# A three-layer GCN with attention behind it: the neighbour sums go in sets of 16 steps, without row copies

## The reference

```python
def _conv(x, row, col, edge_type, edge_weight, W, b):
    deg = segment_sum(ones, col); deg_inv_sqrt = where(deg > 0, deg ** -0.5, 0)
    norm = deg_inv_sqrt[row] * deg_inv_sqrt[col] * edge_weight
    xw = einsum('ni,tio->tno', x, W)                 # 4 tables of N x 128
    x_j = xw[edge_type, col] * norm[:, None]
    return leaky_relu(segment_sum(x_j, row, num_segments=N) + b, 0.01)
z1 = _conv(x, ...W1); z2 = _conv(z1, ...W2); z3 = _conv(z2, ...W3)
x = _layernorm(x + (x + z1 + z2 + z3) / 4)
# attention: alpha = leaky_relu(a_src[src] + a_dst[dst], 0.2), softmax over the edges of a dst,
# out = segment_sum(alpha * xp[src]) + bias
x = _layernorm(x + attention(x))
```

## Time and profile before

| | |
|---|---|
| median of the runs | 8943.34 us |
| span of the profiled execution | 11925.3 us |
| POOL busy | 6395.8 us (54%) |
| PE busy / PEld busy | 5307.0 (45%) / 4105.0 us (34%) |
| DVE busy | 4574.2 us (38%) |
| ACT busy | 3992.0 us (33%) |
| gathers of the layers (L737) | 4743 x 946 ns |
| copies g_step (L912) | 5580 x 390 ns |

### The profile page before, as it was taken

One profiled execution on the slowest core, in us unless ns is written; L12 is line 12 of the kernel. 1 busy time (PEld: TensorE's weight loads), 2 busy tenths in 40 slices (PEclk: granted clock), 3 DMA queues, 4 the chain that ended last, 5 costly groups with the idle time before them and its releaser, 6 DMA issues.

```text
span 11925.3 us, 149378 instructions
## 1 busy us (share of the span) xinstructions
PE 5307.0 (45%) x32765; PEld 4105.0 (34%) x32766; DVE 4574.2 (38%) x12940; ACT 3992.0 (33%) x12236; POOL 6395.8 (54%) x6521
## 2 busy tenths in 40 slices
PE   5843434434533434343433434343444444444444
PEld 4632322223322323232322323232344444444444
DVE  9952222222322212222322222222555555555556
ACT  6522222222322222222322222222455454445455
POOL 1656566565456565656466565656344444444443
PEclk9975655656655655565655556555566666666666
DMA  1011111111221111111211111111122222222222
GB/s 47 35 42 43 41 44 43 41 44 41 65 55 44 40 44 40 44 40 44 76 42 44 40 44 40 44 40 44 49 69 70 68 71 69 69 68 69 70 69 65
DMA packets 432687, 612.42 MB, mean 51 GB/s; under 512 B 232038, under 2 KB 249491, under 8 KB 432539
## 3 DMA queue, kind: packets, MB, share of 16 engines
q0 software_dynamic: 208832, 428.96, 13.7%
q1 hardware_dynamic: 223707, 182.02, 4.6%
HBM read 437.29 MB, written 51.28 MB: 41 GB/s over the span
## 4 chain that ended last, share of the span: by engine, by line
another core or an unknown queue 48%; DVE 16%; issue 15%; PE 8%; ACTq 5%; DVEq 4%; ACT 3%; POOL 0%; DMA 0%; POOLq 0%; SPq 0%
DVEq L1604 3%; PE bank L1196 3%; ACT g_step L912 3%; ACTq L896 2%; DVE a_miss L1717 2%; PE wide L1196 2%; DVE g_hot L1620 2%; ACTq L912 1%; DVE acc L1634 1%; DVE a_max L1722 1%; DVE lo_hot L1262 1%; DVE acc L1788 1%; PE bank L1191 1%; DVE v_hot L1387 1%
## 5 line engine op out<-in xcount | busy, mean ns | idle before, releaser
L737 POOL DMA_INDIRECT g_rows<-gcn_table,rec_idx x4743 | 4487.1, 946 | 2894.2 <-ACT g_step L912 1484.6
L912 ACT ACTIVATE g_step<-g_rows,rec_w 128x128 f32 x5580 | 1791.5, 390 | 5679.7 <-remote 4618.4
L762 POOL DMA_INDIRECT a_roll<-gat_table,src_plane x1612 | 1524.6, 946 | 1801.0 <-ACT a_cand L937 1375.4
L1634 DVE TENSOR_TENSOR acc<-acc,bank 128x512 f32 x930 | 637.9, 686 | 3828.8 <-remote 3238.9
L1191 PE MATMUL bank<-zeros 1*128 1x512 bf16 x930 | 490.9, 528 | 2909.9 <-DVE acc L1634 2104.6
L1196 PE MATMUL bank<-g_step,g_hot 128*128 128x128 f32 x7440 | 1621.7, 386 | 128.4 <-issue 50.6
L1196 PEld LDWEIGHTS bank<-g_step,g_hot 128*128 128x128 f32 x7440 | 1391.8, 280 | 487.9 <-issue 487.9
L1222 PE MATMUL bank<-a_msg,a_hot 128*128 128x130 f32 x3608 | 798.9, 389 | 1648.7 <-DVE a_msg L1768 1635.0
L1222 PEld LDWEIGHTS bank<-a_msg,a_hot 128*128 128x128 f32 x3608 | 685.6, 283 | 1786.3 <-DVE a_msg L1768 1452.3
L1191 PEld LDWEIGHTS bank<-zeros 1*128 1x128 bf16 x930 | 89.9, 97 | 3099.0 <-DVE acc L1634 2163.3
L937 ACT ACTIVATE a_cand<-a_miss,a_rows 128x128 f32<-128x128 bf16 x3608 | 1095.9, 386 | 14.9 <-DMA a_rows<-a_roll 8.8
(11 more groups left out here) (272 smaller groups left out, 5880.3 us busy)
## 6 DMA issues: line engine op xcount, KB each, us to landing
a_rows<-a_roll SPq DMA_DIRECT2D x451, 264.0 KB
g_rows<-gcn_table,rec_idx POOLq DMA_INDIRECT x4743
gcn_table<-rows SPq DMA_DIRECT2D x147, 256.0 KB
a_roll<-gat_table,src_plane POOLq DMA_INDIRECT x1612
e_dst<-by_dst_dst SPq DMA_DIRECT2D x451, 2.0 KB
gat_table<-acc SPq DMA_DIRECT2D x7, 462.0 KB
out_x<-xs SPq DMA_DIRECT2D x6, 448.0 KB
gcn_slots<-nothing SPq DMA_DIRECT2D x4, 468.0 KB, 6.8
```

Of the source, the lines that this page charges most:

```text
L737: pool.indirect_dma_start(out=g_rows[:, tile % RING, :], out_offset=None, in_=gcn_tables[layer % 2], in_offset=bass.IndirectOffsetOnAxis(a ...
L762: pool.indirect_dma_start(out=a_roll[:, g % ROLL, t, :], out_offset=None, in_=gat_table, in_offset=bass.IndirectOffsetOnAxis(ap=src_plane[ ...
L912: last = nc.scalar.activation(g_step[:, j, k, :].unsqueeze(1), g_rows[:, bass.ds(slots[k], 1), :], ACT.Copy, scale=rec_w[:, bass.ds(q.at(0 ...
L1634: V.tensor_tensor(dst_ap, dst_ap, sums_of(j).rearrange("p (k d) -> p k d", k=GP), ALU.add).then_inc(s_gadd, 1)
```

## The change

1. **Sets of 16.** The regular part of a layer now runs in sets of SG = 4 groups, 16 steps. A set's sums lie over four PSUM banks, low or wide, two sets in turn; the columns in gcn_at (partition 64) count from the set's first block instead of the group's. TensorE posts s_gpe once per set, behind four short matmuls of zeros that close the banks; VectorE adds a set in four pieces of 128 x 512.
2. **No row copies.** TensorE reads the gathered rows in the ring g_rows itself. It waits for s_land, and loads tile, ring places and columns from three partitions of gcn_at. ScalarE's copies and g_step are gone; the ring is freed by s_gpe, so by whole sets: POOL's count of needed steps is rounded up to 16.
3. **Weights in the masks.** A step's mask is one instruction of 128 columns, (iota == rec_lo) * rec_w, all of it in SBUF; rec_lo is FP32 now. g_hot has eight groups instead of three.
4. **The endings.** From DONE_FROM = 448 on, 14 groups of four steps run as before, in three single banks, with the next layer's products between them. Their masks are made up to four groups ahead.
5. RB is 116 instead of 117, so that a chunk is 464 steps, 29 sets. The attention layer's lists share gcn_at's memory; acc is exactly 49 blocks long, and the first block of a set is capped so that 16 blocks fit.

```diff
-RB = 117
+RB = 116
-GRP = Turns(ALL_GROUPS - 3, 9)
-ADDS = GRP.steps + 1
+SG = 4
+SUP = Turns(DONE_FROM // SG, 2)
+SSTEPS = SG * GP
+ADDS = ALL_GROUPS - 2 + 1
...
+        super_sums = [low[:, :], wide[:, :, :, :, :].rearrange("p w h t e -> p (w h t e)")]
...
                         if q >= RING_TURNS:
-                            wait_apart(pool, s_copied, layer * GRP.steps - (-steps // GP), s_apart)
+                            wait_apart(pool, s_gpe, layer * POSTS - (-steps // SSTEPS), s_apart)
...
-                    for k in range(GP):
-                        last = nc.scalar.activation(g_step[:, j, k, :].unsqueeze(1),
-                                                    g_rows[:, bass.ds(slots[k], 1), :],
-                                                    ACT.Copy, scale=rec_w[:, bass.ds(q.at(0, GP, k), 1)])
-                    last.then_inc(s_copied, 1)
...
+                def rows_at(group, steps):
+                    tile = pe.value_load(gcn_at[0:1, group, 1], min_val=0, max_val=CH * CCOLS - 1)
+                    _, slots = nc.values_load_multi_w_load_instructions(
+                        gcn_at[32:33, group, 0:GP].rearrange("p g k -> p (g k)"),
...
+                    _, places = nc.values_load_multi_w_load_instructions(
+                        gcn_at[64:65, group, 0:GP].rearrange("p g k -> p (g k)"),
...
+                def products_of(sums, masks, masked_by, values, closing):
+                    tile, slots, places = values
+                    pe.wait_ge(s_ghot, masked_by)
+                    pe.wait_ge(s_land, tile + (CH * CCOLS * layer + 1))
+                    for k in range(GP):
+                        last = nc.tensor.matmul(sums[:, bass.ds(places[k], D)], g_hot[:, masks, k, :],
+                                                g_rows[:, bass.ds(slots[k], 1), :].rearrange("p o d -> p (o d)"),
+                                                start=False, stop=closing and k == GP - 1)
+                    return last
 
                 def body(q):
...
+                    values = rows_at(bass.ds(q.at(0, SG), 1), SSTEPS)
+                    for k in range(SG):
+                        if q.live(-2):
+                            pe.wait_ge(s_gadd, q.at(-2, SG, ADDS * layer + k + 2))
+                        fill(super_sums[j][:, k * GP * D:(k + 1) * GP * D])
+                    for k in range(SG):
+                        now = values
+                        if k + 1 < SG:
+                            values = rows_at(bass.ds(q.at(0, SG, k + 1), 1), SSTEPS)
+                        products_of(super_sums[j], SG * j + k, q.at(0, SG, (ADDS - 1) * layer + k + 1), now,
+                                           False)
+                    for k in range(SG):
+                        last = nc.tensor.matmul(super_sums[j][:, k * GP * D:k * GP * D + 1],
+                                                zeros[0:1, 0:1].to_broadcast([1, P]), zeros[0:1, 0:1],
+                                                start=False, stop=True)
+                    last.then_inc(s_gpe, 1)
+
+                def ending(n):
...
+                    values = rows_at(slice(group, group + 1), GP)
...
+                    fill(sums_of(n))
...
+                    if n < NBATCH and layer < 2:
+                        if n >= 1:
                             products(n - 1)
+                        turn(n)
...
-                        V.tensor_tensor(g_hot[:, j, :, :], spread(iota_ps.unsqueeze(1), [P, GP, P]),
-                                        spread(lo.unsqueeze(2), [P, GP, P]), ALU.is_equal).then_inc(s_ghot, 1)
...
+                    for k in range(GP):
+                        at = bass.ds(step + k, 1)
+                        last = V.scalar_tensor_tensor(g_hot[:, slot, k, :], iota[:, :], rec_lo[:, at],
+                                                      spread(rec_w[:, at], [P, P]), ALU.is_equal, ALU.mult)
+                    last.then_inc(s_ghot, 1)
...
+                def body(q):
+                    if q.live(1):
...
+                            dve.wait_ge(s_gpe, q.at(-1, 1, POSTS * layer + 1))
+                        for k in range(SG):
+                            masks(SG * q.slot(1) + k, q.at(1, SSTEPS, k * GP))
...
+                        dve.wait_ge(s_gpe, q.at(0, 1, POSTS * layer + 1))
+                        dve.wait_ge(s_gadd, q.at(0, SG, adds + 1))
+                        for k in range(SG):
...
+                            V.tensor_tensor(dst_ap, dst_ap, sums.rearrange("p (k d) -> p k d", k=GP), ALU.add
+                                            ).then_inc(s_gadd, 1)
```

More of the change, by code:

```diff
@@ L719, in _ @@
                 if layer:
[L720 removed]
+                    pool.wait_ge(s_gpe, layer * POSTS)
                 for q in range(SORT.steps):
@@ L1161, in products, with fill @@
                                          start=True, stop=True).then_inc(s_tm, 1)
+                def rows_at(group, steps):
+                    tile = pe.value_load(gcn_at[0:1, group, 1], min_val=0, max_val=CH * CCOLS - 1)
+                    _, slots = nc.values_load_multi_w_load_instructions(
+                        gcn_at[32:33, group, 0:GP].rearrange("p g k -> p (g k)"),
+                        engines=(mybir.EngineType.PE,), min_val=0, max_val=RING - 1,
+                        skip_runtime_bounds_check_because="a tile modulo the ring")
+                    _, places = nc.values_load_multi_w_load_instructions(
+                        gcn_at[64:65, group, 0:GP].rearrange("p g k -> p (g k)"),
+                        engines=(mybir.EngineType.PE,), min_val=0, max_val=(steps - 1) * D,
+                        skip_runtime_bounds_check_because="a block less its first, at most one per step")
+                    return tile, slots, places
+                def fill(sums):
+                    nc.tensor.matmul(sums, zeros[0:1, 0:1].to_broadcast([1, P]),
+                                     zeros[0:1, 0:1].to_broadcast([1, GP * D]), start=True, stop=False)
+                def products_of(sums, masks, masked_by, values, closing):
[7 more added lines that the diff above has]
+                    return last
                 def body(q):
@@ L1178, in body @@
                         products(n - 1)
[L1180 to L1199 removed]
+                if layer:
+                    pe.wait_ge(s_gadd, ADDS * layer)
+                    pe.wait_ge(s_tr, (layer + 1) * NB)
+                    pe.wait_ge(s_tc, turns(layer, NBATCH - 1) + 1)
+                run_steps(pe, SUP, 2, 0, body)
+                for n in range(ENDING):
+                    ending(n)
             pe.wait_ge(s_idx, CH)
```

225 lines of the change are left out of this document (97 added, 128 removed).

## The result

The changed kernel takes 9583.17 us (median) against 8943.12: a ratio of 1.0707, with a 95% interval of 1.069 to 1.0724. The forecast was 9100, its range 8860 to 9330. The direction was right, the size was not: +640 us in place of +157. Three of its four runs took 9561.60 to 9586.30 us, and the ratio is theirs; the fourth took 12965.49 at a mean granted clock of 0.277 (0.61 in the others), there is no trace of it, and it stays unexplained.

A forecast was written before the change was run, and what follows sets the result against it. POOL's stream of gathers at a pitch of 1.25 us was taken as the bound. Start 16, masks 94 and endings 47 summed to +157 on the median 8943: 9100 us, range 8860 to 9330 for 8 in 10.

The forecast's parts named there:

- What bounds the kernel: POOL issues 6448 gathers at 1.25 us almost without a break: 8060 us, 8751 with the start, against the median 8943.
- the late posts: TensorE's semaphores reaching VectorE and ScalarE late; claimed to belong to the profiled execution, since other runs end 2982 us sooner.
- The masks, +94: VectorE's two-input masks delay POOL's gathers by 0.28 us a set, a waiting gather getting in between two: +94 us.
- 0.21 us of hold per mask: Stretch from its start for which a 128-column two-input VectorE mask was taken to hold back a gather.
- 0.96 to 1.02: Sign of the forecast: mean duration in us to which the layers' gathers would rise from 946 ns.
- rival 3: Mask bursts shut POOL out to their end (+1200) or TensorE falls behind (+1780); half the first gives 9540; chance 0.13.
- Rival 2: Masks don't hold POOL and loads run under TensorE's work; only the start is left, about 8955 us; chance 0.17.
- its premise on the attention layer: Gathers beside the tiny two-input instructions of the attention layer keep their 946 ns mean.
- Rival 4 (faster): POOL's pitch is below 1.25 us unprofiled and some of 1484.6 us of waits are real; half gives 8780; chance 0.20.
- The first fill, +16: POOL's 43.75 us stop before the 94th tile grows by 7 to 27 us, taken as +16, once.
- The ring in sets of 16, hidden: Freeing the gathered rows by sets: TensorE's 15 us a set stay hidden behind POOL's 17.4.
- The endings' loads, +47: In each layer's last 14 groups, three TensorE number loads leave 1.2 us bare per batch: +47 us (0 to 94).

The follow-up runs named there:

- b_again3: Kernel before with ScalarE's and SyncE's number loads split in two, on a chip with posts on time: 8943.87 us against 8943.16, ratio 1.0001.
- a_ts: Changed kernel with each mask as one TENSOR_SCALAR, only iota streamed from SBUF, on a chip with late posts: 12180.69 us, ratio 1.0111.
- a_ts2: Changed kernel with each mask as one TENSOR_SCALAR, only iota streamed from SBUF, posts on time: 9043.79 us, ratio 1.0113.
- b_iota4: Kernel before with masks as four back-to-back 128-column comparisons with two SBUF inputs, on a chip with late posts: 12291.32 us.
- b_iota: Kernel before with only the masks' iota read from SBUF instead of PSUM, on a chip with late posts: 12131.81 us.
- a_act: Changed kernel with the sets' masks made by ScalarE instead of VectorE, on a chip with late posts: 12254.78 us, ratio 1.0157.
- a_act2: Changed kernel with the sets' masks made by ScalarE, on another chip with late posts: 12245.77 us, ratio 1.0163.
- a_early: Changed kernel with the endings' number loads ahead of the transposes, on a chip with late posts: 12022.25 us, ratio 0.9987.
- b_again: Kernel before with ScalarE's and SyncE's number loads split in two, on a chip with late posts: 12247.71 us against 12060.28, ratio 1.0148.
- a_act3: Changed kernel with the sets' masks made by ScalarE alone, posts on time: 9005.53 us, ratio 1.0068.

## Why the prediction was wrong

The two on-time profiles (b_again3 and the changed kernel), in POOL's time, with the first and last gather of each stretch:

| stretch | before | changed | difference |
|---|---|---|---|
| start to the first gather | 693.3 | 692.0 | -1.3 |
| three layers, first to last gather | 2017.1 + 2013.8 + 2014.4 | 2210.5 + 2203.8 + 2211.8 | +580.8 |
| two turns between layers | 29.3 + 29.3 | 49.7 + 46.7 | +37.8 |
| to the attention layer | 61.7 | 68.5 | +6.8 |
| attention gathers | 2011.2 | 2011.4 | +0.2 |
| behind the last gather | 73.4 | 84.1 | +10.7 |

The sum is +635, of which 580 are the gathers' excess (590.3 against 10.3).

- *What bounds the kernel: right.* POOL's gathers at a pitch of 1.25 us are the kernel. b_again3 shows the pitch of the earlier trace rows (0.94 and 0.30) with the time beside it, and 2014 us for the 1612 gathers of a layer. Making the sum in POOL's time and not in the disturbed span was right too. Only the reason I gave for the late posts was not: on two chips every run of the kernel before takes 12048 to 12060 us, and every profile from there has them.
- *The masks, +94: the step that failed.* The parts were measured as forecast: 0.262 us from mask to mask for my 0.26, a burst of 4.28 for 4.2, 2.2 gathers starting in each (732 in 333 bursts, since a held one leaves room for fewer) for 3.3. What failed is the sentence "I take the +94, as the row nearest to it does: four single-input instructions back to back from 723.15 delayed the gather within them by only 0.09, so a waiting gather gets in between two". That row was the nearest in shape, and of the wrong kind: a_ts and a_ts2 show that single-input instructions hold no gather over 1.15 us even 16 in a row. It could say nothing on what happens between two instructions with two inputs, and nothing on a burst of 16: b_iota4's four were nearly harmless. Per set the loss is 590 / 336 = 1.76 us for my 0.28. The 0.21 us of hold per mask was mis-read too: I took a fixed stretch from the instruction's start, but both long gathers of the earlier trace rows already end 0.8 behind the instruction's end (707.98 + 0.64 + 0.82 = 709.44 = 708.19 + 1.25; for L1549 it is 0.79). The gathers' mean of 1062 ns lies between my 0.96 to 1.02 and the 1.1 that I had set as rival 3's sign.
- *Rival 3 came true, in its half.* I had priced it at +1200 in full and 9540 for a half, and it is 9583. In the trace the half is this: the first gather in a burst passes, and 333 of the 399 later ones wait for its end. Why the first gets through is not shown. I gave it 0.13 on the strength of the same 0.09.
- *Rival 2* falls with the excess, though its premise on the attention layer held: its gathers keep their 944 ns. The Trainium skill ("SBUF — State Buffer", section "Who interferes with whom") lets an instruction with two SBUF inputs shut out a GpSimd one that reads SBUF for its whole length; b_iota and the ends 0.82 behind agree. Its remark that tensor_tensor left GpSimd's DMAs alone does not hold here: b_iota's excess is 112.7 us against 0.6.
- *Rival 4 (faster)* falls: on time, POOL waits 2.4 us for g_step in all. A post that is late on TensorE is worth nothing where no post is late. Nor is the gain that the earlier trace rows seemed to promise seen where they are: a_act, a_act2 and a_ts, with sets of 16 and nearly undisturbed gathers, are 1.1 to 1.6% slower than before there. a_early, whose gathers lose 539 us, is level with before (0.9987), so on those chips the gathers' excess doesn't decide the time. What does is open.
- *The first fill, +16: nothing.* The stop of 43.75 us in the earlier trace rows was a late post; on time neither kernel stops there.
- *The ring in sets of 16, hidden: right.* POOL waits for no set. TensorE waits for rows instead (the two largest of its waits in the changed kernel):

```profile
PE wide L1153 <- POOLq L717: 1346.5, 530, 5.4
PE low L1153 <- POOLq L717: 1175.6, 409, 15.0
```

- *The endings' loads, +47: 36 to 39,* seen where I said, in the turns: I forecast 16 us each and they grew by 20.4 and 17.4, to the attention layer by 6.8. While POOL stands there, TensorE is no longer busy without a break (windows over the first turn, of b_again3 and of the changed kernel: PE 26.01 of 28 us, then 38.57 of 48):

```profile
2711.00:2739.00 28.00, 26.01 (x98) 13.36 (x96) 21.83 (x24) 17.60 (x34) 0.31 (x1) 1.00 0.60 215
```

```profile
2903.00:2951.00 48.00, 38.57 (x142) 20.50 (x141) 30.10 (x44) 19.25 (x28) 0.39 (x1) 0.96 0.46 166
```

- *Left open:* the 10.7 us behind the last gather. The code there is the same, and the on-time runs show 73 to 89 us for it. That the chips differ, I didn't explain.

## What to carry to other kernels

Where GpSimd's gathers are the bound, count for each VectorE instruction beside them how many streamed SBUF inputs it has, and how long such instructions follow each other without a gap: one input (a scalar column in place of a broadcast tensor) cost 11 ns a mask here, two in bursts of 16 cost 106, and the 1395 masks of 512 columns with iota in PSUM cost nothing that shows (0.6 us in b_again). To price a change, don't extend the nearest row across the property that matters; a row of single-input instructions bounds nothing for two-input ones, and a term whose bounds are 0 and +1200 deserves a range that holds its middle. And read a profile's large waits against the runs' time before calling them part of the kernel.

## What the runs showed of the hardware

- A gather delayed by a two-input VectorE instruction ends 0.81 to 0.83 us behind the end of that instruction, of the one in the burst behind which it gets in, or of the whole burst, whatever its own start: 454 of 454 in b_iota, 623 of the 675 over 0.97 us in the changed kernel. In a gapless burst of 128-column instructions the share of gathers over 1.15 us grows with the burst: 20 of 677 (4 comparisons), 68 of 1359 (4 masks), 270 of 1030 (8), 333 of 732 (16). With 0.16 us between two masks there is none (0 of 1162).
- The clearing of acc has no input, and yet a gather lasted 7.08 us over it, and the next but one 6.51 over the masks behind it (POOL and VectorE of the changed kernel):

```profile
2953.32 7.08 POOL L740 DMA_INDIRECT g_rows<-gcn_table,first_idx  x1 [0.30 <-issue]
2954.16 5.29 DVE L1628 MEMSET acc<- 128x6272 f32 x1 [1.37 <-issue]
2959.37 8.36 DVE L1634 SCALAR_TENSOR_TENSOR g_hot<-iota,rec_lo,rec_w 128x128 f32<-128x128 f32 x32
2962.02 6.51 POOL L740 DMA_INDIRECT g_rows<-gcn_table,first_idx  x1 [0.30 <-issue]
```

  In a_ts2, where single-input masks follow the clearing, the same gather takes 7.03. In a_act3 no mask follows it, and the gathers beside it take 0.95:

```profile
2765.96 5.29 DVE L1652 MEMSET acc<- 128x6272 f32 x1 [1.37 <-issue]
2766.44 0.95 POOL L741 DMA_INDIRECT g_rows<-gcn_table,first_idx  x1 [0.31 <-issue]
```

  The kernel before shows the same. With iota in PSUM its clearing (5.61 us in b_again3, masks right behind it) leaves the gathers at 0.94; with iota in SBUF and nothing else changed (b_iota) the gather beside it takes 7.48:

```profile
2741.49 5.61 DVE L1608 MEMSET acc<- 128x6656 f32 x1 [1.45 <-issue]
2742.20 0.94 POOL L733 DMA_INDIRECT g_rows<-gcn_table,first_idx  x1 [0.30 <-issue]
```

```profile
3352.78 7.48 POOL L733 DMA_INDIRECT g_rows<-gcn_table,first_idx  x1 [0.30 <-issue]
3353.30 5.61 DVE L1608 MEMSET acc<- 128x6656 f32 x1 [1.45 <-issue]
```

  So the instruction that stands ready behind a long one counts too. In the changed kernel it is six gathers and 35 of the 590 us.
- On two chips the kernel before took 12048 and 12060 us in every run, 35% above the 8942 to 8943 of the others. There 388 of VectorE's waits ahead of its adds are put down as remote and last 11.0 us on average (b_again); on time the 922 waits for TensorE's sums in bank last 2.9 (b_again3). On those two, splitting ScalarE's and SyncE's loads cost 1.5%; on time it cost nothing (1.0001). The cause is open.
